# Gated cross-attention block: second batch's tokens loaded earlier, four block sums moved to GpSimd

## What is computed

```python
def xattn(t, ctx):                         # t = layernorm(x)
    query, key = ctx @ Wq.T + bq, ctx @ Wk.T + bk
    attention = softmax(query @ key.T)
    return t @ attention.T
def ternary_quant(w):
    scale = mean(abs(w)) + 1e-8
    return clip(round(w / scale), -1, 1) * scale
def ffn(t):
    return (silu(t @ wu.T) * (t @ wg.T)) @ wd.T   # wu, wg, wd: ternary_quant of the weights
x = x + tanh(g_xattn[0]) * xattn(layernorm(x), ctx)
x = x + tanh(g_ffn[0]) * ffn(layernorm(x))
```

## Time and profile before

| quantity | value |
|---|---|
| median of 3 executions | 412.23 us (411.55 to 412.46) |
| profiled execution, its own time | 412.31 us |
| its span, first to last instruction | 410.5 us |
| outside of the span | 1.81 us |
| TensorE matmuls (PE), busy | 391.2 us, 95% |
| VectorE (DVE) | 316.2 us, 77% |
| ScalarE (ACT) | 267.3 us, 65% |
| GpSimd (POOL) | 173.6 us, 42% |
| mean granted TensorE clock | 0.983 |

### The profile page before, as it was taken

The page is one execution under the profiler, slowest core; times in us unless marked ns, Lnnn a source line. Parts: engine busy times, 40 slices in busy tenths (PEclk is TensorE's granted clock), DMA queues, the critical chain, the costliest instruction groups (busy, mean ns, idle before and its releaser), DMA issues.

```text
span 410.5 us, 6058 instructions
## 1 busy us (share of the span) xinstructions
PE 391.2 (95%) x1944; PEld 215.5 (52%) x1952; DVE 316.2 (77%) x473; ACT 267.3 (65%) x360; POOL 173.6 (42%) x189
## 2 busy tenths in 40 slices
PE   8999079989999999999999999999999999999997
PEld 6576057544444444444444444444444656656886
DVE  1866268588888998478888886577869998798984
ACT  3887166867987878686898875466277775564400
POOL 0850871965798502240406300535356574461000
PEclk9999669999999999999999999999999999999999
DMA  8999912729960003002002963024230000000014
GB/s 300 414 417 401 405 60 44 173 99 255 215 172 20 0 1 104 0 14 91 0 2 66 192 116 76 15 77 129 102 103 2 2 2 0 2 2 0 2 51 155
DMA packets 43183, 43.91 MB, mean 107 GB/s; under 512 B 30992, under 2 KB 33168, under 8 KB 41104
## 3 DMA queue, kind: packets, MB, share of 16 engines
q1 hardware_dynamic: 43152, 43.53, 34.2%
HBM read 29.89 MB, written 6.29 MB: 88 GB/s over the span
## 4 chain that ended last, share of the span: by engine, by line
PE 76%; DMA 5%; DVE 5%; POOL 5%; issue 5%; ACT 2%; SPq 1%; DVEq 0%; POOLq 0%; ACTq 0%
PE pair L870 22%; PE pair L872 22%; PE pair L944 13%; PE pair L988 11%; DMA xb_lo<-in_xT 5%; PE pair L763 3%; PE pair L786 2%; POOL xf L594 1%; DVE small L1471 1%; DMA xf<-in_first 1%; POOL small L568 1%; PE pair L736 1%; DVE xf L1674 1%; ACT sh L1100 1%; SPq L400 1%
## 5 line engine op out<-in xcount | busy, mean ns | idle before, releaser
L870 PE MATMUL pair<-xb_hi,w_sb 128*128 128x512 f16 x448 | 169.8, 379 | 0.2 <-DVE xf L1669 0.2
L872 PE MATMUL pair<-xb_lo,w_sb 128*128 128x512 f16 x448 | 169.8, 379 | 0.0
L870 PEld LDWEIGHTS pair<-xb_hi,w_sb 128*128 128x128 bf16 x448 | 43.9, 98 | 52.5 <-ACT xf L1297 0.7
L872 PEld LDWEIGHTS pair<-xb_lo,w_sb 128*128 128x128 bf16 x448 | 43.9, 98 | 51.1 <-issue 0.3
L1248 ACT ACTIVATE xf<-xf,small 128x512 f32<-128x512 f32 x48 | 34.5, 720 | 52.4 <-DVE xf L1669 31.6
L944 PE MATMUL pair<-x_sb,sh 128*128 128x512 bf16 x248 | 55.1, 379 | 0.4
L1674 DVE SCALAR_TENSOR_TENSOR xf<-xf,small 128x512 f32<-128x512 f32 x48 | 40.0, 836 | 8.4 <-ACT xf L1248 8.4
L944 PEld LDWEIGHTS pair<-x_sb,sh 128*128 128x128 f16 x256 | 24.8, 98 | 30.7 <-DVE x_sb L1711 0.9
L607 POOL TENSOR_TENSOR w_sb<-w_sb 128x512 bf16<-128x512 bf16 x8 | 9.6, 1196 | 63.1 <-ACT w_sb L1122 63.1
L1679 DVE TENSOR_TENSOR sh<-xf,sh 128x512 f16<-128x512 f32 x36 | 32.1, 899 | 0.7 <-ACT sh L1259 0.7
L1725 DVE SCALAR_TENSOR_TENSOR x_sb<-pair,small,x_sb 128x256 f32<-128x256 f32 (+1 forms) x57 | 25.5, 474 | 5.9 <-PE pair L988 5.4
(11 more groups left out here) (199 smaller groups left out, 731.5 us busy)
## 6 DMA issues: line engine op xcount, KB each, us to landing
w_sb<-in_wugT SPq DMA_DIRECT2D x8, 1024.0 KB, 14.0
x_sb<-in_x SPq DMA_DIRECT2D x4, 1024.0 KB, 12.0
xf<-in_wdT SPq DMA_DIRECT2D x4, 1024.0 KB, 7.0
xt_sb<-in_wdT SPq DMA_DIRECT2D x4, 1024.0 KB, 4.8
xt_sb<-in_xT SPq DMA_DIRECT2D x12, 256.0 KB, 5.7
x_dram<-x_sb SPq DMA_DIRECT2D x8, 256.0 KB, 3.3
out<-x_sb SPq DMA_DIRECT2D x8, 256.0 KB, 2.0
x_sb<-x_dram SPq DMA_DIRECT2D x2, 1024.0 KB, 6.1
```

Of the source, the lines that this page charges most:

```text
L870: pe.matmul(dst[:, m * 512:(m + 1) * 512], w[:, o:o + P], hi[:, k], start=start and k == 0, stop=False, skip_group_check=not start)
L872: last = pe.matmul(dst[:, m * 512:(m + 1) * 512], w[:, o:o + P], lo[:, k], start=False, stop=k == 1, skip_group_check=not start)
```

## The change

It does three things. SyncE's list issues xT of batch 1 in two pairs of tiles, ahead of up 2 and behind it, and so ahead of context 2 and of the wait in it. `norm_x1` of batch 1 moves from GpSimd to VectorE (around `low_t(0, "B21")`), counted by `s_x2n` instead of `s_x2p`. T3, T1, T2 and T4 of the first pair move from VectorE to GpSimd: T3 ahead of `rstd2(2, 0)`, T1 ahead of `rstd2(2, 1)`, T2 ahead of `rstd2(2, 2)`, T4 ahead of `sum_1(0)`. The rest of the diff is the counts of the semaphore.

```diff
@@ SyncE @@
             load_ug(0, 1)
+            load_xt(1, 0)
+            load_xt(1, 1)
             load_ug(0, 2)
+            load_xt(1, 2)
+            load_xt(1, 3)
             load_ctx(2)
             load_ug(0, 3)
-            load_ug(1, 0)
-            for i in range(NT):
-                load_xt(1, i)
-                if i < 3:
-                    load_ug(1, i + 1)
+            for c in range(NABS):
+                load_ug(1, c)
@@ GpSimd @@
             rstd1(2, 1)
-            for h in range(2):
-                rstd2_two(1, h)
-                norm_x1(1, 2 * h)
-                norm_x1(1, 2 * h + 1)
+            rstd2_two(1, 0)
+            rstd2_two(1, 1)
+            hold(pool, s_x2n, 2 * NT)
+            pool.tensor_tensor(t3_sb, xf_half(1, 1), xf_half(1, 0), ALU.subtract).then_inc(s_t3, 1)
             for b in range(NS, NB - 1):
                 for i in range(NT):
+                    if i == 1:
+                        hold(pool, s_t3, 1)
+                        pool.tensor_tensor(xf_half(1, 0), xf_half(1, 0), xf_half(0, 0), ALU.subtract).then_inc(s_t1, 1)
+                    if i == 2:
+                        hold(pool, s_t1, 1)
+                        hold(pool, s_tl, t_done(0, "B11"))
+                        pool.tensor_tensor(xf_half(0, 0), t3_sb, xf_half(0, 0), ALU.add).then_inc(s_t2, 1)
                     rstd2(b, i)
...
             rstd1(NB - 1, 2)
+            hold(pool, s_tl, t_done(0, "B21"))
+            hold(pool, s_t2, 1)
+            pool.tensor_tensor(xf_half(0, 1), xf_half(0, 1), xf_half(0, 0), ALU.subtract).then_inc(s_t4, 1)
             sum_1(0)
@@ ScalarE @@
                             high_t(0, "T2", xf_half(0, 0))
-                            act.wait_ge(s_x2p, NT)
+                            act.wait_ge(s_x2n, 2 * NT)
                             high_t(0, "B22", xf_half(1, 1))
@@ VectorE, end of b = 1 @@
                 else:
+                    norm_x1(1, 0)
+                    norm_x1(1, 1)
                     low_t(0, "B21", xf_half(0, 1))
+                    norm_x1(1, 2)
+                    norm_x1(1, 3)
@@ VectorE, b = 2 and 3 @@
-                    if last and i == NT - 1:
-                        hold(dve, s_tl, t_done(0, "B21"))
-                        hold(dve, s_t2, 1)
-                        dve.tensor_tensor(xf_half(0, 1), xf_half(0, 1), xf_half(0, 0), ALU.subtract).then_inc(s_t4, 1)
...
                     if b == 2:
-                        if i == 0:
-                            hold(dve, s_x2p, NT)
-                            dve.tensor_tensor(t3_sb, xf_half(1, 1), xf_half(1, 0), ALU.subtract).then_inc(s_t3, 1)
-                            hold(dve, s_t3, 1)
-                            dve.tensor_tensor(xf_half(1, 0), xf_half(1, 0), xf_half(0, 0), ALU.subtract)\
-                                .then_inc(s_t1, 1)
                         if i == 1:
                             low_t(0, "T3", t3_sb)
                         if i == 2:
                             low_t(0, "T1", xf_half(1, 0))
-                        if i == 3:
-                            hold(dve, s_t1, 1)
-                            hold(dve, s_tl, t_done(0, "B11"))
-                            dve.tensor_tensor(xf_half(0, 0), t3_sb, xf_half(0, 0), ALU.add).then_inc(s_t2, 1)
```

More of the change, by code:

```diff
@@ L150, in gated_block_kernel @@
         s_half = sem("s_half")
-        s_ss, s_ts, s_mp, s_xe, s_x2p = (sem(n) for n in ("s_ss", "s_ts", "s_mp", "s_xe", "s_x2p"))
+        s_ss, s_ts, s_mp, s_xe = (sem(n) for n in ("s_ss", "s_ts", "s_mp", "s_xe"))
         s_dt, s_ev, s_shift = sem("s_dt"), sem("s_ev"), sem("s_shift")
@@ L589, in p_sums_2 @@
                 pool.tensor_tensor(p_sum(b, 3), p_quarter(b, 1, 0), p_sum(b, 1), ALU.subtract).then_inc(s_ts, 1)
[L591 to L595, removed]
             def rstd2(b, i):
@@ L1318, in sign_down @@
                 act.wait_ge(d_spill, 16 * 8)
-                act.wait_ge(s_x2n, NG - NT if c > 1 else 2 * NT)
+                act.wait_ge(s_x2n, NG if c > 1 else 3 * NT)
                 act.activation(t_d[:, c * ACOLS:(c + 1) * ACOLS], xt_flat[:, :], ACT.Sign, bias=nmagic).then_inc(s_tda, 1)
@@ L1383, in _ @@
                     act.wait_ge(s_td, 4)
-                    act.wait_ge(s_x2n, NG - NT)
+                    act.wait_ge(s_x2n, NG)
                     high_t(NU, "B11", xf_half(2, 0))
@@ L1803, in _ @@
                     norm_x1(NB - 1, 3)
-                    hold(dve, s_x2n, NG - NT)
+                    hold(dve, s_x2n, NG)
                     dve.wait_ge(d_tb["T4"], d_tb_done(0, "T4"))
```

## The result

The changed kernel takes 400.8 us (median of 4, 400.43 to 400.83), the kernel before 412.35 on the same chip; the ratio is 0.9719, with a 95% interval of 0.9702 to 0.9737. The profiled execution has a span of 399.0 us. The forecast was 399.4 us with a range of 398.4 to 402.3.

What follows compares the result with a forecast made beforehand. Bound: TensorE's 11.93 us hole, behind the late xT of batch 1. Hole -10.66, clock -2.44 and T1 on GpSimd +0.3 make -12.8 us: 412.31 to 399.5, given as 399.4 us for the median, range 398.4 to 402.3.

Steps and rivals of the forecast that it cites:

- What bounds it: TensorE's 11.93 us hole before batch 1's second product, traced through GpSimd to the late landing of batch 1's xT.
- part 1: Earlier loads of batch 1's xT let TensorE start again at 43.25 instead of 53.91 us: -10.66 us.
- VectorE's statistics as the next late thing: On GpSimd, rstd1_two(1, 1) would wait for statistics that VectorE ends at 38.42 us; L582 then runs at 41.85.
- the landing by bytes: Batch 1's xT, at 8.91 MB in the queue, lands at 26.1 us, 1.8 us of offset included.
- The clock: After the shortened hole the clock stays at 1.00; the two products take 3.62 instead of 6.06 us: -2.44 us.
- the other case: Rival: the clock falls despite the short hole, or the hole stays over 3 us: 401.8 us, chance 0.08.
- ScalarE's cover: Gate sums (1, 2) and (1, 3) end 2.7 us late beside TensorE's products; costed at nothing, up to 1 us.
- Part 2: Batch 1 normalized by VectorE in a 3 us hole, 8.3 us off GpSimd: nothing on the path.
- Part 3: Block sums on GpSimd: T1 delays ScalarE's exp_row(3, 2) from 87.96 to 88.3, +0.3 us; bounds -0.5 and +2.
- T1 as the next late thing: On GpSimd T1 ends at 87.1 us old time, where VectorE had it at 85.82, holding ScalarE before exp_row(3, 2).
- The step that failed: The second phase lasts as long as before; T4 moves sum_1(0)'s end to 109, hidden before product 5 at 112.8.
- The port rival: GpSimd's sums meet VectorE's two-input operations, T2 against norm_x1(2, 2) and low_t(T1): 2.6 us, 402.0 us, chance 0.12.

Runs made afterwards that it cites:

- e7: The changed kernel with all four xT tiles of batch 1 directly behind gate 0 in the load queue: 406.23 us, ratio 0.9845 to the kernel before.
- e8: The changed kernel with all four xT tiles of batch 1 directly behind gate 1 in the load queue: 408.35 us, ratio 0.9898 to the kernel before.
- e5: The changed kernel with GpSimd's p_sums_1(1) ahead of rstd1_two(1, 1) and rstd2_two(0, 1): 402.36 us, ratio 0.9759 to the kernel before.
- e3: The changed kernel with T3, T1, T2 and T4 back on VectorE, batch 1 still normalized there: 399.1 us, ratio 0.9665 to the kernel before.
- e1: The kernel before with the new order of the loads alone: 400.71 us, ratio 0.9705 to the kernel before.
- e4: The changed kernel with T1 on GpSimd directly behind rstd2(2, 0), ahead of rstd1(2, 2) and the coefficients: 399.55 us, ratio 0.9678 to the kernel before.
- e2: The changed kernel with the old order of the loads, only normalization and the four sums moved: 413.2 us, ratio 1.0012 to the kernel before.

## Why the prediction was right, and where not

- **What bounds it, and part 1**: right. The hole went from 11.93 to 1.55 us. I had -10.66; measured from the first product of batch 1 the second one starts 15.53 us later before and 5.15 after: -10.38. Of the 0.28 missing 0.20 is in GpSimd's steps from the statistics to L583, 3.53 us (39.11 to 42.64) instead of 3.33: L559 and L560 took 0.36 and 0.81 us where the same two took 0.19 and 0.77 before. Another 0.06 is in the handing over, 0.16 us instead of 0.1. VectorE's statistics as the next late thing, the landing by bytes, and 13.6 us from there to TensorE are shown by the rows above, e7 and e8.
- **The clock**: right, -2.37 (5.90 to 3.53 us) for the forecast -2.44. e5 shows how near the other case was: in its profiled execution a hole of 2.09 us took the clock down and cost some 1.7 us on top, and two of its four executions kept the clock at 1.000.
- **ScalarE's cover**: I cost the later gate sums at nothing; the products behind took 29.95 us to the next short hole, 30.00 before. Right.
- **Part 2** I cost at nothing on the path. It is worth 1.34 us (e3 against e1), hidden in the changed kernel by T1. I had seen that VectorE comes 3 us earlier to make_x1(2, 1), and that T1's lateness uses it up.
- **Part 3**: T1 as the next late thing is right and shown by e3 and e4. It ended 1.2 us later against the second phase than before (22.34 us ahead of it instead of 23.51); I had 1.3. Together parts 2 and 3 made -0.08 us of the stretch for the forecast +0.3. The stretch in all: -12.82 for -12.8. That it fits to 0.02 us is luck: the hole and the clock gave 0.35 less than I had, and the short holes and parts 2 and 3 cost as much less.
- **The step that failed** is the sentence that the second phase goes on as long as before once "ScalarE, VectorE and the transposes come along", with T4 ahead of the weight sums as "hidden". The term was put at nothing and measured +0.80. I counted its cover at product 5 only, where TensorE is late by 0.1 us. Further on the weight sums come 2.2 us later and meet two VectorE instructions, which take 1.45 and 1.64 us instead of 0.77 and 0.74; VectorE is 0.82 us late from there, and TensorE after it. The port rival of the prediction (GpSimd's sums beside VectorE's two-input operations) comes nearest to it, but I had priced it at another place, and at 2.6 us.
- The other 0.5 us lie ahead of the change's first effect. By the 14 profiles this is chance; it makes nearly all of the rest of the difference between 399.4 and 400.8.

The Trainium skill (Perfetto Trace Analysis, "Optimizing Scalar/DVE Operations") warns that moving work from VectorE to GpSimd might not help, because of the read port that they share. The outcome agrees: with the sums on VectorE again the kernel is faster (e3, 0.9665 against 0.9719). The reason is another in the first phase, where T1's place in the list made the loss (e4, with T1 on GpSimd still but sooner, has 0.9678). For the 0.8 us of the second phase a shared port would fit, since the slow instructions ran beside GpSimd's sums; no run isolates it.

## What to carry to other kernels

Look for the earliest long hole of the busiest engine and follow it back to what landed last; bytes ahead of a load in a saturated queue, with one landing of the old kernel to set the offset (1.8 us here), told when it lands to about a microsecond, and so how far forward it must move. When a hole is closed to a microsecond or two, the order of the lists around it decides what is left, and a reordering that only shifts the hole can cost more than it gives, through the clock. Count work moved to another engine in that engine's list: what stands behind it, who waits there, and what it locks out.

## What the runs showed that I had not expected

- The clock's price did not grow with the hole: the two products behind it took 3.53 us after a hole of 1.55, 6.43 after 4.51, 5.56 after 6.59, 5.90 after 11.93 (before) and 6.48 after 11.90 (e2). The last two tell how much one execution differs from another behind the same hole, so the order of the other two is not shown to be the holes' doing.
- GpSimd's 128x1024 sums took 2.35 to 2.37 us in the first phase, where the earlier trace rows had 2.62 and 2.87.
- A single norm_x1 of 0.55 us took 2.47 when T1 had started 0.17 us before it.
